# Four layers of attention with relative positions on one core: score blocks of 512 columns, a ring of PSUM banks for each reading engine, and the weighted sums of two tiles in one run

## The reference, cut to what matters

```
attn  = softmax(q k' / 4 + rel_h[query, key row] + rel_w[query, key column])   # 2304 x 2304 per head
out   = (attn @ v) @ proj_w + proj_b
rel_h = q . Rh[row distance],  rel_w = q . Rw[column distance]
```

## Time and profile before

| | |
|---|---|
| median of 3 runs | 7578.99 us (7577.27 to 7584.46) |
| profiled execution, its own time | 7594.71 us |
| its span in the profile | 7592.9 us |
| PE busy in the span | 7277.3 us (96%) |
| PEld busy | 4560.6 us (60%) |
| DVE busy | 5487.1 us (72%) |
| ACT busy | 4915.2 us (65%) |
| DMA queue q1, share of 16 engines | 58.1% |

### The profile page before, as it was taken

How to read it: one execution, slowest core, us unless ns; L and a number is a source line. 1 busy time by engine, 2 the same in 40 slices (tenths; PEclk the granted TensorE clock), 3 DMA queues, 4 the chain that set the end, 5 groups by cost and what they waited for, 6 DMA issues and landing times.

```text
span 7592.9 us, 148674 instructions
## 1 busy us (share of the span) xinstructions
PE 7277.3 (96%) x57632; PEld 4560.6 (60%) x57632; DVE 5487.1 (72%) x10165; ACT 4915.2 (65%) x11761; POOL 932.2 (12%) x966
## 2 busy tenths in 40 slices
PE   7999999999999999999999999999999999999998
PEld 4656656666666665656656566566666666656564
DVE  5777777767777677776777777777777767777773
ACT  1666666666666666666666666666666666666665
POOL 2111001120101100011101111011101021101010
PEclk7999999999999999999999999999999999999999
DMA  5556565555565656656565655666555655565553
GB/s 136 115 138 145 127 132 134 138 139 128 133 142 132 150 121 139 138 133 140 121 136 136 146 134 131 130 144 142 129 133 134 141 140 139 122 142 135 130 129 92
DMA packets 270732, 1014.29 MB, mean 134 GB/s; under 512 B 102544, under 2 KB 155216, under 8 KB 174160
## 3 DMA queue, kind: packets, MB, share of 16 engines
q1 hardware_dynamic: 270032, 1004.79, 58.1%
HBM read 745.26 MB, written 255.69 MB: 132 GB/s over the span
## 4 chain that ended last, share of the span: by engine, by line
PE 89%; DMA 4%; issue 2%; DVE 2%; SPq 1%; POOL 1%; ACT 0%; POOLq 0%; ACTq 0%; DVEq 0%
PE work L724 29%; PE work L804 26%; PE work L789 24%; PE work L735 5%; DMA qk_scratch<-back 2%; PE work L773 2%; PE work L754 1%; DMA moving<-rel_scratch 1%; PE work L762 1%; DVE mpart L624 1%; POOL back L477 0%; SPq L310 0%; DVE xb L615 0%; PE work L741 0%; POOL split_hi L475 0%
## 5 line engine op out<-in xcount | busy, mean ns | idle before, releaser
L624 DVE TENSOR_REDUCE mpart<-work 128x1 f32<-128x512 f32 (+1 forms) x8640 | 5087.0, 631 | 1767.6 <-PE work L724 1747.0
L549 ACT ACTIVATE probs<-work 128x384 f32<-128x384 f32 x10368 | 4381.2, 494 | 2334.2 <-PE work L804 2302.7
L804 PE MATMUL work<-moving,keys 113*128 113x384 f32 x10368 | 3769.3, 368 | 172.0 <-issue 140.4
L724 PE MATMUL work<-mkeys,hi 128*128 128x512 f32 (+1 forms) x8640 | 3548.1, 412 | 72.2 <-ACT back L537 43.5
L724 PEld LDWEIGHTS work<-mkeys,hi 128*128 128x128 f32 x8640 | 1670.5, 193 | 1294.3 <-issue 703.6
L804 PEld LDWEIGHTS work<-moving,keys 113*128 113x128 f32 x10368 | 1978.4, 193 | 566.4 <-ACT probs L549 230.9
L789 PE MATMUL work<-probs,vall 128*17 128x288 f32 x27648 | 2059.4, 416 | 0.6 <-ACT probs L549 0.6
L789 PEld LDWEIGHTS work<-probs,vall 128*17 128x17 f32 x27648 | 644.0, 98 | 924.3 <-ACT probs L549 403.6
L462 POOL TENSOR_TENSOR full<-full,hi 128x384 f32<-128x384 f32 x576 | 578.1, 1004 | 1706.2 <-DVE hi L667 1706.2
L467 POOL TENSOR_TENSOR rden<-oraw,rden 128x576 f32<-128x576 f32 x96 | 137.0, 1427 | 4415.9 <-DMA rden<-inverse_scratch 4415.9
L735 PEld LDWEIGHTS work<-image,tab 128*48 128x48 f32 x9216 | 604.9, 127 | 68.1 <-issue 3.8
(11 more groups left out here) (42 smaller groups left out, 641.2 us busy)
## 6 DMA issues: line engine op xcount, KB each, us to landing
moving<-rel_scratch SPq DMA_DIRECT2D x1728, 144.0 KB
moving<-qk_scratch SPq DMA_DIRECT2D x288, 576.0 KB
rel_scratch<-hi SPq DMA_DIRECT2D x192, 432.0 KB, 5.5
rel_scratch<-full SPq DMA_DIRECT2D x192, 432.0 KB, 5.7
moving<-rel_scratch SPq DMA_DIRECT2D x288, 288.0 KB
image<-qk_scratch SPq DMA_DIRECT2D x96, 576.0 KB, 5.7
keys<-qk_scratch SPq DMA_DIRECT2D x192, 288.0 KB, 4.6
qk_scratch<-split_hi SPq DMA_DIRECT2D x144, 192.0 KB, 3.2
```

What stands on the lines that cost most here:

```text
L549: act.activation(probs[:, tile % RING, i * BLK:(i + 1) * BLK], score[:, (6 * tile + i) % BANKS, 0:BLK], ACT.Exp).then_inc(score_read, 1)
L624: dve.tensor_reduce(mpart[:, u % 2, q, m:m + 1], bank[:, 0:min(512, N - 512 * m)], AX.X, ALU.max)\
L724: pe.matmul(bank[:, 0:w], hi[:, u % 2, q * P:(q + 1) * P], mkeys[:, u % 2, 512 * m:512 * m + w], start=True, stop=True).then_inc(for_dve, 1)
L804: pe.matmul(score[:, n % BANKS, 0:BLK], tile_of(keys[0:K_ROWS, u % 2, :], c, third), moving[0:K_ROWS, slot, i * BLK:(i + 1) * BLK], start= ...
```

## The change

- Score blocks: five of 256, 512, 512, 512, 512 columns instead of six of 384 (`SPLIT`). The max matmuls are cut in the same way, so that the one of 256 columns now comes first.
- Rings: `score` (three banks) now takes all that ACT reads, scores, rel, mt and q/k items, in PE's order; `aux` (three banks) all that DVE reads. Semaphores for filled and read are one pair for each ring; `score_filled` and `score_read` go.
- Order: a slot's items are issued ahead of the slot's score block, not behind it. The rel item and the late items move from slot 5 to slot 0 of the same tile: rel ahead of the max item, the late item behind it. Max items stand in slots 0, 1, 2, 4 and 5. There is no score block in slot 5.
- Sums: `attend` is issued for two tiles in one run, at the end (slot 5, behind the last max item) of every even tile t: the sums of tiles t - 2 and t - 1. `sums_out` moves to tile 1, slot 0, behind the first max item.

```diff
-ATTEND_AT = 4
+SPLIT = [(0, 256)] + [(512 * i + 256, 512 * i + 768) for i in range(4)]
+SB = len(SPLIT)
+MSPLIT = SPLIT
+MAX_AT = (0, 1, 2, 4, 5)
...
-                    plan[u][t][m].append(("max", n, q, m))
+                    plan[u][t][MAX_AT[m]].append(("max", n, q, m))
             if t < 12 and u + 2 < UNITS:
-                plan[u][t][5].append(("rel", u + 2, t))
+                plan[u][t][0].insert(0, ("rel", u + 2, t))
...
-                plan[u][12 + k][5].append(item)
+                plan[u][12 + k][0].append(item)
...
-ON_ACT = ("rel", "mt", "qk")
+ON_ACT = ("score", "rel", "mt", "qk")
...
             def fill(item):
-                n, _ = place[item]
-                bank = aux[:, n % BANKS, :]
+                n = place[item]
+                on_act = item[0] in ON_ACT
+                bank = (score if on_act else aux)[:, n % BANKS, :]
+                if item[0] == "score":
+                    ready_for_scores(item[1], item[2])
                 if n >= BANKS:
-                    before = order[n - BANKS]
-                    pe.wait_ge(act_read if before[0] in ON_ACT else dve_read, place[before][1])
-                if item[0] == "max":
+                    pe.wait_ge(act_read if on_act else dve_read, n - BANKS + 1)
+                if item[0] == "score":
+                    _, tile, i = item
+                    u, t = divmod(tile, TILES)
+                    c, third = divmod(t, THIRDS)
+                    lo, up = SPLIT[i]
+                    pe.matmul(bank[:, 0:up - lo], tile_of(keys[0:K_ROWS, u % 2, :], c, third),
+                              moving[0:K_ROWS, slot_of(u, third)[0], lo:up], start=True, stop=True).then_inc(for_act, 1)
...
-                        if u >= 1 and (t, i) == (0, 5) and u <= UNITS:
+                        if u >= 1 and (t, i) == (1, 0) and u <= UNITS:
                             sums_out(u - 1)
...
-                    for i in range(6):
-                        if 0 <= u < UNITS:
-                            scores(tile, i)
-                        if i == ATTEND_AT and 0 < tile <= TILES * UNITS:
-                            attend(tile - 1)
+                    for i in range(SB + 1):
                         for item in plan[u][t][i]:
                             fill(item)
+                        if i == SB and t % 2 == 0 and 0 < tile <= TILES * UNITS:
+                            attend(tile - 2)
+                            attend(tile - 1)
+                        if 0 <= u < UNITS and i < SB:
+                            fill(("score", tile, i))
```

More of the change, by code:

```diff
@@ L217, in slot_of, with scored @@
             return slot, use
+        def scored(tile):
+            return place["score", tile, SB - 1] + 1
         def tile_of(ap, c, third):
@@ L512, in consume @@
             def consume(item):
-                n, count = place[item]
-                bank = aux[:, n % BANKS, :]
-                act.wait_ge(for_act, count)
-                if item[0] == "rel":
+                n = place[item]
+                bank = score[:, n % BANKS, :]
+                act.wait_ge(for_act, n + 1)
+                if item[0] == "score":
+                    _, tile, i = item
+                    lo, up = SPLIT[i]
+                    if i == 0 and tile >= RING:
+                        act.wait_ge(attended, tile - RING + 1)
+                    act.activation(probs[:, tile % RING, lo:up], bank[:, 0:up - lo], ACT.Exp).then_inc(act_read, 1)
+                elif item[0] == "rel":
                     rel_out(item[1], item[2], bank)
@@ L542, in _ @@
                 for t in range(TILES):
-                    for i in range(6):
-                        if 0 <= u < UNITS:
-                            tile = TILES * u + t
-                            if i == 0 and tile >= RING:
-                                act.wait_ge(attended, tile - RING + 1)
-                            act.wait_ge(score_filled, 6 * tile + i + 1)
-                            act.activation(probs[:, tile % RING, i * BLK:(i + 1) * BLK],
-                                           score[:, (6 * tile + i) % BANKS, 0:BLK], ACT.Exp).then_inc(score_read, 1)
+                    for i in range(SB + 1):
                         for item in plan[u][t][i]:
@@ L553, in _ @@
                                 consume(item)
+                        if 0 <= u < UNITS and i < SB:
+                            consume(("score", TILES * u + t, i))
         @block.vector
@@ L661, in high @@
                 cols = slice(r * BLK, (r + 1) * BLK)
-                dve.wait_ge(act_read, place["rel", u, 7 + r // 2 * 2][1])
+                dve.wait_ge(act_read, place["rel", u, 7 + r // 2 * 2] + 1)
                 if r == 0:
```

99 lines of the change are left out of this document (48 added, 51 removed).

## The result

| | before | changed |
|---|---|---|
| median of 4 runs | 7578.13 us | 7455.18 us (7436.85 to 7472.1) |
| ratio | | 0.9836, 95% interval 0.9806 to 0.9865 |
| span of the profiled execution | 7592.9 us | 7470.3 us |

The change makes the kernel 1.6% faster. The forecast was 7230 us with 7080 to 7430 as its range; the sign was right, the gain 2.8 times too large, and the measured time lies above the range.

A forecast was written before the change was run, and what follows sets the result against it. PE, busy 96%, was taken as the bound, with DMAs pacing unit ends. Savings of 3.6 us a unit gave 343 us over 95 units, plus some 5 for the last: 350 us off, so 7230 us, range 7080 to 7430.

The forecast's parts named there:

- Score blocks cost nothing: Score blocks on PE: 1.04 us a tile as six of 384, 1.05 as the new five, so no gain or loss.
- The rule on weight loads: Rival: each score block shows a bare weight load, so one block fewer saves 123 us more, 7105 us; chance 0.03.
- Change-over of 0.32 us, and 0.06 more ahead of a rel item: Pairing sums saves one PE change-over, 0.32 us for two tiles, and 0.06 us more where a rel matmul follows.
- Bank waits: PE's waits for readers' banks in tile pairs, from 0.1 to 0.9 us a pair; 2.6 us in twelve tiles.
- The end of the unit: DMA-paced stretch from tile 13: the rel store comes earlier and the end moves with it, -1.5 us (bounds 0 and -2.7).
- Plain units: Units without late items, j = 9, 10, 11 and 0: -3.1 us a unit in all.
- Under which DVE catches up, so a pair saves its 0.32 and its present waits: Units j = 1, 2, 7: late items take 1.29 us of PE; three pairs save 2.5 us, -4.5 a unit; j = 8 -3.9.
- The late item in tile 12 hides its waits: Units j = 4 to 6: the late item covers tile 12's bank waits, making the gain -3.5 us a unit.
- a late item ahead of its score block is the same work: Small moves: issuing a late item ahead of its score block leaves the work the same.
- j = 3: Units with group norm, counted with the units without late work: -3.1 us a unit.
- the slower one: Rival: DVE's ring paces PE after each run of sums; slower from 6.2 us of waits a unit; chance 0.07.
- drain anew: Rival: the second tile of a run drains again, or reduces keep a 0.68 us pitch; 7430 us; chance 0.10.

The follow-up runs named there:

- run 10: Changed kernel with sums of one tile at the end of every tile and six score blocks of 384 columns; 7469.66 us, ratio 0.9831.
- runs 13 and 14: Changed kernel (13), and with one tile's sums every tile (14), DVE and ACT reading only 128 columns of each block; 7124.54 and 7209.6 us.
- the order alone: Kernel before with only the new order and one tile's sums at the end of every tile; old blocks and rings; 7574.68 us, ratio 0.9975.
- run 6: Changed kernel with tile 16's sums at the end of tile 17, only tile 17's at the end of next tile 0; 7408.94 us, ratio 0.9758.
- run 7: Changed kernel, paired sums kept, with DVE reducing only the first 128 columns of each max block; 7262.35 us, ratio 0.9570.
- run 5: Changed kernel with late items in slot 5, behind the last max item and ahead of the sums, instead of slot 0; 7382.25 us, ratio 0.9728.
- run 15: Changed kernel with sums of one tile at the end of every tile and late items in slot 5; 7185.2 us, ratio 0.9465.
- run 1: Changed kernel with late items of even tiles in slot 3, where no max item is, instead of slot 0; 7485.3 us, ratio 0.9866.
- run 2: Changed kernel with single sums: one tile's at the end of every tile instead of two at the end of every other; 7315.26 us, ratio 0.9638.

## Why the prediction was wrong, point by point

The miss is the gain that three kinds of units did not give: those with q/k items, with projection or v items, and with group norm statistics. Another wrong step, that the blocks are worth nothing, erred the other way and hid part of it.

- *Score blocks cost nothing.* Wrong. The PE sum, 1.04 against 1.05 us, is right, but a block also sets when its reader's bank comes free. The small block first and the wider ones give 1.9% with single sums, and the small max block first 1.3%. The rule on weight loads of the Trainium skill (TensorE: Matmul & The Clock Gate, Part 3), kept as a rival, does not explain it: the trace has loads beside matmuls (2678.40 under 2678.29, run 10), except after a wait.
- *Change-over of 0.32 us, and 0.06 more ahead of a rel item.* The size is right without a rel item (0.32 between runs 13 and 14). With one it is 0.26: the narrow load is a gain of the order, which single sums have in every tile, and was booked to the pairing.
- *Bank waits.* The ledger was right in kind and nearly in size. Forecast and measured pairs of plain units: (1,2) 8.16 and 8.05, (3,4) 7.41 and 7.40, (5,6) 7.41 and 7.62, (7,8) 7.46 and 7.63, (9,10) 7.68 and 7.62, (11,12) 7.64 and 7.25. What the prediction did not ask is whether the pairing is worth these waits. It is not: single sums have hardly any in tiles 3 to 10 (7.56 us a pair, 7.52 with both readers short), and are 2.0% faster.
- *The end of the unit.* Right in mechanism: the store comes earlier and the end moves with it, 1.8 us for 1.5. But this belongs to sums behind the last score block, not to pairs: single sums and the order alone have it too. The sums owed after the wait, and the lower clock that meets them, were not costed; they take 0.8% of the kernel's time (run 6).
- *Plain units, -3.1 foreseen and -2.9 measured.* In part this is luck. With single sums the same units fall by 5.7 us, so the pairing costs 2.8 us there, and the blocks and the order, which had been given far less, pay for it.
- *"Under which DVE catches up, so a pair saves its 0.32 and its present waits".* **This step failed in units j = 1, 2, 7 and 8.** Each of the pairs behind tile 12 was to save some 0.8 us. In j = 1, 2 and 7 (means), (11,12) takes 9.3 us for 8.7, (13,14) 10.2 for 10.1 and (15,16) 9.4 for 9.4, and only (17,0) falls, 8.1 for 9.5. The waits are on DVE's banks: with short reduces these units give the forecast gain (-4.4 for -4.5, run 7). The item's place, just behind the sums where DVE has no backlog, is the smaller part: slot 5 gives 0.7 us with pairs (run 5) and nothing with single sums (run 15), and single sums give 1.4 us. The term was also too large by its own numbers: 0.32 and 2 x (4.86 - 3.39 - 1.29) make 0.68 us a pair and 2.0 for three pairs, not 2.5.
- *"The late item in tile 12 hides its waits" for j = 4 to 6, and "a late item ahead of its score block is the same work".* **This step failed and is the largest part of the miss**: +0.6 us for -3.5. It is the same work on PE, but on ACT it puts the wait for POOL's split ahead of the tile's exponentials. ACT's waits for that split are 88.6 us in the kernel before, 187.6 in the changed one, and 97.1 with the items in slot 5, where the units come down by 2.6 us, and by 4.6 with single sums. Short reduces give 1.4 us of it.
- *j = 3.* -3.1 foreseen, +1.7 measured. DVE's statistics stand in tiles 0 to 11, and pairs (3,4) take 7.99 us with them against 7.41 without; before it was 7.79 with or without. The prediction left them out. **This term failed too**: with short reduces the unit falls by 5.3 us, to 3.7 below the kernel before.
- *The whole.* Against the measured 1.17 us a unit, the foreseen 3.6 miss 29.1 us a stage: 12.1 in j = 4 to 6, 7.5 in j = 1, 2, 7, 4.8 in j = 3, 2.4 in j = 8, 1.8 in j = 0 and 0.5 in the rest.
- The rivals: the slower one had a right place, DVE's ring (ACT's is the other), but not the price that it needed. The run of two tiles did not drain anew (0.97 us for its second sixteen records), and the DMAs did come earlier. The pairing in the kernel before shows what it looks like when it decides: 4.1% slower.

**Open.** Why units j = 0 gain less than the other plain ones. They scatter from 73 to 81 us by stage in the changed kernel, and fell to a mean of 74.5 in run 1, which moved nothing in them. Open too is how far the q/k stall is the order of stores in SP's queue, and which part of the 0.8% of run 6 is the clock in units other than the one shown.

## What to carry to other kernels

When two engines drain PE's banks, do not put a long run that fills no bank where a shorter one would do, unless the readers are fast: here the saved change-over (0.26 to 0.32 us for two tiles) was less than what the readers' idle time cost PE afterwards, and with both readers cut short the long run won by 1.1%. A moved item has a price for each queue that it stands in, so ask what its reader has to do at that moment; the q/k items did best behind the tile's other blocks, right ahead of a run that fills no bank. And try the smallest block first after such a run, for its bank is the first that PE will ask for (0.9% and 1.3% here).

## What was not expected of the hardware

- In the case shown in run 10 a wait of PE for a bank costs more than its length: the weight load that follows it, 0.11 us for 128 columns, stands bare. A wait of some 0.05 us cost 0.16. In run 2's kernel the load waits as well, but under a longer matmul, and costs nothing.
- In the sums, which go to four groups of columns, two tiles in a row run without a seam: 32 records take 2.06 us, so 1.09 for the first sixteen with its way in and out, and 0.97 for the next.
- At the boundary of the units the granted clock was 0.83 on the mean of 10 us where PE had waited 2.60 us, and 1.00 where it had waited 0.55; it was at its lower level, 0.50, from 2839 to 2842, and sums of two tiles stretched from 2.13 to 2.79 us.
